# State-space stage: the first eight projected blocks in another order, the second group's decay masks built later, and its two segment halves parted by a projection

## The chip, the cores and the metric

The kernel runs on one core of one Trainium2 chip. The metric is the device time of one execution in microseconds (us). Five engines work side by side and meet only through semaphores: TensorE (PE in the profile), VectorE (DVE), ScalarE (ACT), GpSimd (POOL) and SyncE (SP), which here issues the loads.

## What is computed

A perceiver layer on 128 latent tokens of width 512: cross-attention, then a state-space (Mamba-2-like) mixer, then a sparse feed-forward, each behind a layer norm and a residual. The change lies wholly in the beginning of the mixer, whose reference reads, cut to what matters:

```python
proj = hidden_states @ in_proj_w.T              # gate 8192, x 8192, B 1024, C 1024, dt 128 columns
xc = conv_general_dilated(hBC, conv_w, ...) + conv_b      # 4 taps, per channel
hBC = silu(xc)                                            # x, B, C come out of this
dt = softplus(dt + dt_bias)
Lmat = exp(segment_sum(A * dt))                           # per head, 128 x 128, causal
Gm = einsum('bclhn,bcshn->bclsh', Cch, Bch)               # C times B, one for each of 8 groups
M = Gm * Lmat
Y_diag = einsum('bclsh,bcshp->bclhp', M, x * dt)
y = Y_diag + D * x
y = rmsnorm(y) * norm_w * silu(gate)
return y @ out_proj_w.T
```

With 128 tokens there is one chunk, so no state is carried over. There are 8 groups of 16 heads; one group has 1024 columns of x and 1024 of gate.

## The kernel before, in words

Everything is kept transposed (channels on partitions, tokens along the free axis). The input projection is done in **blocks** of 4 x 128 output channels (32 matmul records in the profile). A block is one slot of a ring of six weight buffers (1 MB each), loaded by SP in the order of use, and it goes into PSUM bank 0 or 1 in turn. `in_proj` (L1467) waits for its weights and for `proj_ev`, which ScalarE counts up each time it has read a block out of its bank, so a block can start when the block two before it has been read.

The mixer starts with a prologue of eight blocks, whose rows of the weight matrix are listed in `FIRST_IN`: group 0's two gate blocks and two x blocks, two B blocks and two C blocks (B and C serve all groups). From then on each group takes four blocks, which hold the x and gate of the next group: `project(g, j)` with j = 0, 1 for x and j = 2, 3 for gate.

What the other engines do with a block:

- A gate block: ScalarE applies silu from PSUM into `sg` (`gate_out`, L721).
- An x, B or C block: ScalarE copies it to `raw` and writes the last tap with the bias into `acc` (`raw_out`, L524 and four times L710); VectorE adds the other three taps with twelve instructions (`conv`, L1056) that read `raw` and `acc` in SBUF and then counts `taps` up; ScalarE applies silu into `xc` or `bc` (`conv_silu`, L717) and counts `silu_ok` up. There are two `raw`/`acc` pairs.

Decays of a group g: GpSimd writes the group's `a = A*dt` masked by causality into `at_hi`/`at_lo` with two selects (`steps_a(g)`, L499), PE sums them along the segment by a product with a triangular matrix, half a group (8 heads) at a time into banks 2 and 3 (`segments(g, b, half)`, L1478/L1479), ScalarE takes the exponential (`decay_exp`, L726), and VectorE multiplies with `gm` (`mask_decay`, L1071). There is one pair of banks, so a `segments` waits for the `decay_exp` of the one before it. `gm` is the product of C and B (PE, L1527, then masked on VectorE, L1113); it needs all six convolutions of the prologue (`silu_ok` 6).

`x_transposes(g)` (L1487) turns x to tokens on partitions in banks 4 and 5, VectorE scales it by dt (`x_times_dt`, L1076), `y_product(g)` (L1496) writes y over the same banks, and VectorE adds `D*x` (`skip_add`, L1084) and counts `y_ok` up, which the next `x_transposes` waits for. ScalarE squares y for the norm (`squares`, L733), VectorE multiplies it with the gate (`gated`, L1092), and `out_proj` (L1507) projects.

The order on every engine is the order of the code; nothing is scheduled by a planner. ScalarE's exp and silu lie in different function tables, and an `ACT_TABLE_LOAD` stands wherever it passes from one to the other. The first two groups are written out by hand, since the pipeline fills there; from group 1 on every engine runs `mamba_step`.

Of the kernel before, what the change touches and what calls it, by code (L numbers as in the profile page):

```python
# [22 lines left out]
ACT = mybir.ActivationFunctionType  # L23
# [3 lines left out]
T = 128  # L27
# [68 lines left out]
def build(nc, x, ctx_t, wq, wk, wv, wo, w_in, w_dt, w_out, conv_w, conv_b, dt_bias, a_log, d_skip,  # L96
          norm_w, c1, c2, w1, w2, w2_tail, out):
    with ExitStack() as ctx:
# [74 lines left out]
        with ExitStack() as st3:  # L173
# [24 lines left out]
            with ExitStack() as st4:  # L198
# [14 lines left out]
                raw = [sbuf(st4, f"raw{b}", [P, 4, T]) for b in range(2)]  # L213
                acc = [sbuf(st4, f"acc{b}", [P, 4, T]) for b in range(2)]
                xc = [sbuf(st4, "xc0", [P, TPG, T])]
# [66 lines left out]
        def stream(m):  # L282


            slot = (m + 2) % RING
            return slot, BEFORE[slot] + m // RING

        FIRST_IN = (0, 1, 16, 17, 32, 33, 34, 35)

        def step_chunk(g, j):  # L290

            slot, before = stream(8 + j)
            return slot, before + g
# [129 lines left out]
        def _(pool):  # L423
# [72 lines left out]
            def steps_a(g):  # L496

                for dst, src in ((at_hi[g % 2], a_hi), (at_lo[g % 2], a_lo)):
                    i = pool.affine_select(  # L499
                        out=dst[:], in_=src[:, g * HPG:g * HPG + HPG].bitcast(F32).unsqueeze(2).to_broadcast([P, HPG, T]),  # L500
                        compare_op=ALU.is_ge, fill=0.0, base=0, pattern=[[0, HPG], [1, T]],
                        channel_multiplier=-1)
                i.then_inc(at_ok, 1)
# [3 lines left out]
            pool.memset(c2_sb[:], 0.0).then_inc(zeroed, 1)  # L507
            pool.wait_ge(a_ok, 2)
            steps_a(0)
            steps_a(1)  # L510
            for g in range(GROUPS - 2):
                pool.wait_ge(seg_ps, 2 * g + 4)
# [10 lines left out]
        def _(act):  # L523
# [174 lines left out]
            act.wait_ge(const_in, 128)  # L698
            nc.scalar.activation(softplus[5][:], alog[:], ACT.Exp).then_inc(a_ok, 1)

            def raw_out(chunk, k, bank, tile):


                act.wait_ge(freed[chunk[0]], chunk[1] + 1)
                if not (isinstance(k, int) and k < 2):
                    act.wait_ge(taps, k - 1)
                    act.wait_ge(silu_ok, k - 1)
                copy(raw[bank][:], ps[:, bank, :].rearrange("p (c t) -> p c t", c=4))
                for i in range(4):
                    ins = nc.scalar.activation(acc[bank][:, i, :], ps[:, bank, i * T:i * T + T], ACT.Identity,  # L710
                                               bias=cb[:, bass.ds(tile + i, 1)],
                                               scale=cw[:, bass.ds(tile + i, 1), 3:4].rearrange("p a b -> p (a b)"))
                ins.then_inc(proj_ev, 1)

            def conv_silu(k, slot, dst):
                act.wait_ge(taps, k + 1)
                nc.scalar.activation(dst, acc[slot][:], ACT.Silu).then_inc(silu_ok, 1)  # L717

            def gate_out(chunk, bank, dst):
                act.wait_ge(freed[chunk[0]], chunk[1] + 1)  # L720
                nc.scalar.activation(dst, ps[:, bank, :].rearrange("p (c t) -> p c t", c=4),  # L721
                                     ACT.Silu).then_inc(proj_ev, 1)

            def decay_exp(g, b, half):
                act.wait_ge(seg_ps, 2 * g + half + 1)
                nc.scalar.activation(decay[b][:, 8 * half:8 * half + 8, :],  # L726
                                     ps[:, 2:4, :].rearrange("p a (h t) -> p (a h) t", t=T),
                                     ACT.Exp).then_inc(dec_ok, 1)
# [3 lines left out]
                act.wait_ge(sq_ok, g + 1)  # L732
                nc.scalar.activation(ysq[:], yv[:], ACT.Square).then_inc(ysq_ok, 1)  # L733

            gate_out(stream(0), 0, sg[0][:, 0:4, :])
            gate_out(stream(1), 1, sg[0][:, 4:8, :])
            raw_out(stream(2), 0, 0, 0)
            raw_out(stream(3), 1, 1, 4)
            conv_silu(0, 0, xc[0][:, 0:4, :])
            raw_out(stream(4), 2, 0, 64)  # L740
            conv_silu(1, 1, xc[0][:, 4:8, :])
            raw_out(stream(5), 3, 1, 68)
            conv_silu(2, 0, bc[:, 0:4, :])
            raw_out(stream(6), 4, 0, 72)
            conv_silu(3, 1, bc[:, 4:8, :])
            raw_out(stream(7), 5, 1, 76)
            conv_silu(4, 0, bc[:, 8:12, :])
            conv_silu(5, 1, bc[:, 12:16, :])
            decay_exp(0, 0, 0)

# [3 lines left out]
            raw_out(step_chunk(0, 1), 7, 1, 12)  # L754
            decay_exp(1, 1, 0)
            decay_exp(1, 1, 1)
            gate_out(step_chunk(0, 2), 0, sg[1][:, 0:4, :])
            conv_silu(6, 0, xc[1][:, 0:4, :])
            conv_silu(7, 1, xc[1][:, 4:8, :])
            gate_out(step_chunk(0, 3), 1, sg[1][:, 4:8, :])  # L760
            squares(0)
# [54 lines left out]
        def _(dve):  # L816
# [247 lines left out]
            def taps_of(q, k, slot, tile):  # L1064
                dve.wait_ge(proj_ev, q + 1)
                conv(k, slot, tile)
# [40 lines left out]
                nc.vector.tensor_tensor(sq_sum[:], sq_sum[:], ysq[:], ALU.add).then_inc(sq_ok, 1)  # L1107

            for k, tile in enumerate((0, 4, 64, 68, 72, 76)):
                taps_of(k + 2, k, k % 2, tile)  # L1110
            x_times_dt(0)
            dve.wait_ge(gm_ps, 1)
            nc.vector.tensor_tensor(gm[:], ps[:, 6:8, :].rearrange("p a (g t) -> p (a g) t", t=T),  # L1113
# [100 lines left out]
        def _(pe):  # L1214
# [296 lines left out]
            def project(g, j):  # L1511
                slot, before = step_chunk(g, j)
                in_proj(slot, before + 1, 4 * g + 8 + j, j % 2)
# [7 lines left out]

            x_transposes(0, 0)
            project(0, 0)
            project(0, 1)
            pe.wait_ge(silu_ok, 6)
            for g in range(GROUPS):
                ins = mm(ps[:, 6 + g // 4, (g % 4) * T:(g % 4 + 1) * T], bc[:, g, :], bc[:, 8 + g, :],  # L1527
                         start=True, stop=True)
            ins.then_inc(gm_ps, 1)
            segments(0, 0, 1)  # L1530
            project(0, 2)
            segments(1, 1, 0)
            segments(1, 1, 1)
            y_product(0, 0)
            project(0, 3)
# [142 lines left out]
```

## Time and profile before

| what | value |
|---|---|
| three timed runs | 661.26, 661.22, 659.51 us; median 661.22 |
| the profiled execution | 660.41 us, of it 657.9 us are the profile's span |
| PE busy in the span | 638.9 us, 97% |
| share of PE on the chain that ended last | 86% |
| the mixer, from its first block to the addition to the residual | 396.0 to 625.9 us of the span |

The span is what the records cover; the rest of the execution lies outside the engines' records. PE is the engine of the kernel: what matters is where it stands still, and who ended each standstill. The state-space prologue ends at about 452 us, where PE enters the loop body for group 1.

### The profile page before, as it was taken

Reading aid. Unit: us, or ns where it says so; the run is one execution under the profiler, and the core shown is the slowest. Engines: PE = TensorE matmul, PEld = TensorE weight load, DVE = VectorE, ACT = ScalarE, POOL = GpSimd, SP = SyncE. Lnnn points to the kernel's source line nnn. Section 1 sums busy time; section 2 is a strip of 40 time slices with the busy share of each in tenths; the row PEclk is TensorE's granted clock in tenths of the full one; section 3 lists DMA queues with packets and bytes.
Section 4 is the critical chain, followed back from the end, with each engine's and each line's share of the span. In section 5 each row is a group of like instructions: output and inputs, shape, how many; then the busy total and the mean of one; then the engine's idle time right before and its main releaser. Section 6 shows DMA issues by size and latency. Waiting matters only on the chain.

```text
span 657.9 us, 12479 instructions
## 1 busy us (share of the span) xinstructions
PE 638.9 (97%) x4212; PEld 546.6 (83%) x4212; DVE 451.4 (69%) x1056; ACT 362.3 (55%) x711; POOL 203.9 (31%) x150
## 2 busy tenths in 40 slices
PE   7999999999999999999999999998999999999998
PEld 6888888898899989998999879987788797797473
DVE  3533143787788878787888665979975856758873
ACT  3413115777787778767877744767354444447210
POOL 0000000644674478447755454003320220200000
PEclk9999999999999999999999999999999999999999
DMA  7611002226254442625242656674657658597600
GB/s 254 273 64 62 4 0 69 78 69 196 73 153 121 135 137 73 195 67 193 60 130 67 229 236 166 246 281 151 237 214 269 249 201 298 212 350 294 250 1 16
DMA packets 27224, 104.80 MB, mean 159 GB/s; under 512 B 7424, under 2 KB 7808, under 8 KB 17584
## 3 DMA queue, kind: packets, MB, share of 16 engines
q1 hardware_dynamic: 26608, 103.23, 45.9%
q10 hardware_dynamic: 576, 1.05, 0.5%
q8 instruction: 23, 0.38, 0.2%
q14 instruction: 17, 0.14, 0.1%
HBM read 86.30 MB, written 0.26 MB: 132 GB/s over the span
## 4 chain that ended last, share of the span: by engine, by line
PE 86%; DVE 4%; POOL 4%; ACT 3%; issue 1%; DMA 1%; SPq 0%; ACTq 0%; DVEq 0%
PE ps L1467 19%; PE ps L1225 14%; PE ps L1226 14%; PE ps L1227 14%; PE ps L1507 8%; PE ps L1358 4%; PE ps L1302 3%; POOL pt_lo L430 3%; PE ps L1496 2%; PE ps L1617 2%; PE ps L1580 1%; DVE acc L1056 1%; DMA ring<-wk_dram 1%; POOL k_lo L430 1%; PE ps L1487 1%
## 5 line engine op out<-in xcount | busy, mean ns | idle before, releaser
L1467 PEld LDWEIGHTS ps<-norm_t,ring 128*128 128x128 f32 x1152 | 131.5, 192 | 4.8 <-issue 4.1
L1467 PE MATMUL ps<-norm_t,ring 128*128 128x128 f32 x1152 | 133.1, 276 | 0.0
L1056 DVE SCALAR_TENSOR_TENSOR acc<-raw,cw,acc 128x127 f32<-128x127 f32 (+2 forms) x240 | 85.9, 432 | 23.1 <-ACT acc L710 22.2
L430 POOL TENSOR_TENSOR pt_lo<-far_t,pt_hi 128x512 fp32r<-128x512 f32 (+1 forms) x75 | 87.3, 1183 | 37.9 <-ACT pt_hi L524 37.7
L1225 PE MATMUL ps<-pt_hi,v_hi 128*128 128x256 f32 x272 | 84.6, 311 | 3.0 <-POOL pt_lo L430 2.7
L524 ACT ACTIVATE pt_hi<-ps 128x512 fp32r<-128x512 f32 (+1 forms) x69 | 41.0, 596 | 67.1 <-PE ps L1358 67.0
L1227 PE MATMUL ps<-pt_lo,v_hi 128*128 128x256 f32 x272 | 76.6, 282 | 0.0
L1226 PE MATMUL ps<-pt_hi,v_lo 128*128 128x256 f32 x272 | 76.5, 281 | 0.0
L915 DVE TENSOR_SCALAR_CACHE_REDUCE prob_near<-ps 128x512 f32<-128x512 f32 x64 | 44.2, 691 | 24.4 <-PE ps L1227 22.6
L817 DVE TENSOR_TENSOR pt_lo<-ps,pt_hi 128x512 fp32r<-128x512 f32 (+1 forms) x69 | 47.4, 688 | 18.9 <-ACT pt_hi L524 17.6
L499 POOL TENSOR_SCALAR_AFFINE_SELECT at_hi<-a_hi 128x2048 fp32r<-128x2048 f32 x8 | 17.0, 2130 | 136.6 <-PE ps L1479 125.5
L1225 PE MATMUL ps<-k_hi,q_hi 128*128 128x512 f32 (+1 forms) x160 | 58.7, 367 | 0.7 <-DVE k_lo L817 0.3
L1226 PE MATMUL ps<-k_hi,q_lo 128*128 128x512 f32 (+1 forms) x160 | 59.2, 370 | 0.0
L1227 PE MATMUL ps<-k_lo,q_hi 128*128 128x512 f32 (+1 forms) x160 | 58.7, 367 | 0.0
L915 DVE TENSOR_SCALAR_CACHE_REDUCE prob_far<-ps 128x512 f32<-128x512 f32 (+1 forms) x96 | 51.0, 554 | 11.2 <-PE ps L1227 11.2
L1225 PEld LDWEIGHTS ps<-pt_hi,v_hi 128*128 128x128 f32 x272 | 51.6, 190 | 7.5 <-POOL pt_lo L430 5.4
L430 POOL TENSOR_TENSOR wo_lo<-ring,wo_hi 128x1024 fp32r<-128x1024 f32 x15 | 36.2, 2410 | 66.7 <-ACT wo_hi L524 66.7
L1507 PE MATMUL ps<-ring,ug 128*128 128x512 f32 x128 | 56.7, 594 | 0.0
L430 POOL TENSOR_TENSOR v_lo<-v_all,v_hi 128x768 fp32r<-128x768 f32 (+1 forms) x12 | 20.7, 1752 | 115.8 <-ACT v_hi L524 115.8
L1226 PEld LDWEIGHTS ps<-pt_hi,v_lo 128*128 128x128 f32 x272 | 51.6, 190 | 1.6
L1227 PEld LDWEIGHTS ps<-pt_lo,v_hi 128*128 128x128 f32 x272 | 51.2, 188 | 0.0
L602 ACT ACTIVATE prob_far<-prob_far,neg_max 128x512 f32<-128x512 f32 x64 | 48.9, 767 | 3.4 <-DVE neg_max L919 2.7
(205 smaller groups left out, 1311.0 us busy)
## 6 DMA issues: line engine op xcount, KB each, us to landing
ring<-w_in_dram SPq DMA_DIRECT2D x36, 1024.0 KB, 4.9
far_t<-blocks_t SPq DMA_DIRECT2D x240, 72.0 KB, 2.0
ring<-w_out_dram SPq DMA_DIRECT2D x16, 1024.0 KB, 4.9
ring<-wq_dram SPq DMA_DIRECT2D x8, 1024.0 KB, 5.1
ring<-wo_dram SPq DMA_DIRECT2D x8, 1024.0 KB, 6.9
w_sb<-w_dram SPq DMA_DIRECT2D x4, 896.0 KB, 9.1
ring<-ctx_t_dram SPq DMA_DIRECT2D x3, 1024.0 KB, 6.8
ring<-w_dram SPq DMA_DIRECT2D x3, 1024.0 KB, 8.6
```

The source lines that it names most:

```text
L430: sub = lambda dst, a, hi: pool.tensor_tensor(dst, a, hi, ALU.subtract)
L524: copy = lambda dst, src: nc.scalar.activation(dst, src, ACT.Copy)
L602: nc.scalar.activation(prob(b, h, lo, hi), prob(b, h, lo, hi), ACT.Exp, bias=neg_max[:, b, h:h + 1], accum_out=part_sum[:, b, h, i:i + 1]) ...
L817: sub = lambda dst, a, hi: nc.vector.tensor_tensor(dst, a, hi, ALU.subtract)
L915: nc.vector.tensor_scalar(prob(b, h, lo, hi), ps[:, c % 4, 0:hi - lo], SCALE, None, ALU.mult, ALU.max, accum_out=chunk_max[:, b, h, i:i + ...
L1056: ins = nc.vector.scalar_tensor_tensor(a[:, i, back:], r[:, i, 0:T - back], cw[:, bass.ds(tile + i, 1), 3 - back:4 - back].rearrange("p a ...
L1225: mm(dst, a_hi_, b_hi_, start=first, stop=False)
L1226: mm(dst, a_lo_, b_hi_, start=False, stop=False)
L1227: return mm(dst, a_hi_, b_lo_, start=False, stop=last)
L1358: ins = nc.tensor.transpose(ps[:, 4 + u % 2, at:at + P], prob(b, h, kt * P, kt * P + P), ident[:])
L1467: ins = mm(ps[:, bank, t * T:t * T + T], w[:, t, c, :], norm_t[:, c, :], start=(c == 0), stop=(c == NC - 1))
L1507: ins = mm(ps[:, 6, :], ug[b][:, 4 * i + t, :], w[:, t, :], start=(first and i == 0 and t == 0), stop=(last and i == 1 and t == 3))
```

## The change

Five edits:

1. `FIRST_IN` lists the prologue's blocks in the order x, x, gate, B, B, C, C, gate instead of gate, gate, x, x, B, B, C, C. Banks, ring slots and PE's instructions stay the same. ScalarE's code follows, so `raw_out` now takes the `raw`/`acc` pair and the bank apart (an odd block can be in pair 0).
2. VectorE's convolutions wait for the changed count of blocks read.
3. GpSimd builds group 1's masked steps (`steps_a(1)`) only after the six convolutions of the prologue (`taps` 6).
4. PE computes `gm` and group 0's second segment half before the second x block of group 1 instead of behind it, and group 1's two segment halves have the first gate block of group 1 between them.
5. ScalarE takes `conv_silu(6)` ahead of `gate_out(step_chunk(0, 2))`.

```diff
-        FIRST_IN = (0, 1, 16, 17, 32, 33, 34, 35)
+        FIRST_IN = (16, 17, 0, 32, 33, 34, 35, 1)
...
             steps_a(0)
+            pool.wait_ge(taps, 6)
             steps_a(1)
...
-            gate_out(stream(0), 0, sg[0][:, 0:4, :])
-            gate_out(stream(1), 1, sg[0][:, 4:8, :])
-            raw_out(stream(2), 0, 0, 0)
-            raw_out(stream(3), 1, 1, 4)
+            raw_out(stream(0), 0, 0, 0)
+            raw_out(stream(1), 1, 1, 4)
+            gate_out(stream(2), 0, sg[0][:, 0:4, :])
             conv_silu(0, 0, xc[0][:, 0:4, :])
-            raw_out(stream(4), 2, 0, 64)
+            raw_out(stream(3), 2, 0, 64, 1)
             conv_silu(1, 1, xc[0][:, 4:8, :])
-            raw_out(stream(5), 3, 1, 68)
+            raw_out(stream(4), 3, 1, 68, 0)
             conv_silu(2, 0, bc[:, 0:4, :])
-            raw_out(stream(6), 4, 0, 72)
+            raw_out(stream(5), 4, 0, 72, 1)
             conv_silu(3, 1, bc[:, 4:8, :])
-            raw_out(stream(7), 5, 1, 76)
+            raw_out(stream(6), 5, 1, 76, 0)
             conv_silu(4, 0, bc[:, 8:12, :])
+            gate_out(stream(7), 1, sg[0][:, 4:8, :])
             conv_silu(5, 1, bc[:, 12:16, :])
...
+            conv_silu(6, 0, xc[1][:, 0:4, :])
             gate_out(step_chunk(0, 2), 0, sg[1][:, 0:4, :])
-            conv_silu(6, 0, xc[1][:, 0:4, :])
             conv_silu(7, 1, xc[1][:, 4:8, :])
...
-                taps_of(k + 2, k, k % 2, tile)
+                taps_of(k + (k > 1), k, k % 2, tile)
...
             project(0, 0)
-            project(0, 1)
             pe.wait_ge(silu_ok, 6)
             for g in range(GROUPS):
                 ins = mm(ps[:, 6 + g // 4, (g % 4) * T:(g % 4 + 1) * T], bc[:, g, :], bc[:, 8 + g, :],
                          start=True, stop=True)
             ins.then_inc(gm_ps, 1)
             segments(0, 0, 1)
+            project(0, 1)
+            segments(1, 1, 0)
             project(0, 2)
-            segments(1, 1, 0)
             segments(1, 1, 1)
```

How it moves instructions. First PE, behind the product C times B: `at_hi0` are group 0's masked steps and `at_hi1` group 1's, `ring5` is the second x block of group 1 and `ring0` its first gate block. Before:

```order
L1478 MATMUL ps<-at_hi0,upper_r 128x512 [waits at_ok,dec_ok]
L1479 MATMUL ps<-at_lo0,upper_r 128x512
L1478 MATMUL ps<-at_hi0,upper_r 128x512
L1479 MATMUL ps<-at_lo0,upper_r 128x512
L1467 MATMUL ps<-norm_t,ring0 128x128 [waits proj_ev,landed0]
L1467 MATMUL ps<-norm_t,ring0 128x128 x15
L1478 MATMUL ps<-at_hi1,upper_r 128x512 [waits at_ok,dec_ok]
L1479 MATMUL ps<-at_lo1,upper_r 128x512
L1478 MATMUL ps<-at_hi1,upper_r 128x512
L1479 MATMUL ps<-at_lo1,upper_r 128x512
L1478 MATMUL ps<-at_hi1,upper_r 128x512 [waits at_ok,dec_ok]
L1479 MATMUL ps<-at_lo1,upper_r 128x512
```

and in the changed kernel (its lines have other numbers: L1469 is `in_proj`, L1480 and L1481 are `segments`):

```order
L1481 MATMUL ps<-at_lo0,upper_r 128x512
L1480 MATMUL ps<-at_hi0,upper_r 128x512
L1481 MATMUL ps<-at_lo0,upper_r 128x512
L1469 MATMUL ps<-norm_t,ring5 128x128 [waits proj_ev,landed5]
L1469 MATMUL ps<-norm_t,ring5 128x128 x15
L1480 MATMUL ps<-at_hi1,upper_r 128x512 [waits at_ok,dec_ok]
L1481 MATMUL ps<-at_lo1,upper_r 128x512
L1480 MATMUL ps<-at_hi1,upper_r 128x512
L1481 MATMUL ps<-at_lo1,upper_r 128x512
L1469 MATMUL ps<-norm_t,ring0 128x128 [waits proj_ev,landed0]
L1469 MATMUL ps<-norm_t,ring0 128x128 x15
L1480 MATMUL ps<-at_hi1,upper_r 128x512 [waits at_ok,dec_ok]
```

The block of `ring5` has moved from ahead of the product into the gap between group 0's and group 1's segments, and the block of `ring0` into the gap between the halves of group 1; the two groups of `at_hi1` no longer stand back to back.

Second ScalarE, at the entry of the prologue; `freed2` to `freed5` and `freed0` are the signals that PE is through with the first to fifth block. Before:

```order
L721 ACT_TABLE_LOAD
L721 ACTIVATE sg0<-ps 128x512 [waits freed2]
L721 ACTIVATE sg0<-ps 128x512 [waits freed3]
L524 ACTIVATE raw0<-ps 128x512 [waits freed4]
L710 ACTIVATE acc0<-ps,cb,cw 128x128 x4
L524 ACTIVATE raw1<-ps 128x512 [waits freed5]
L710 ACTIVATE acc1<-ps,cb,cw 128x128 x4
L717 ACTIVATE xc0<-acc0 128x512 [waits taps]
L524 ACTIVATE raw0<-ps 128x512 [waits silu_ok,taps,freed0]
```

and in the changed kernel:

```order
L525 ACTIVATE raw0<-ps 128x512 [waits freed2]
L712 ACTIVATE acc0<-ps,cb,cw 128x128 x4
L525 ACTIVATE raw1<-ps 128x512 [waits freed3]
L712 ACTIVATE acc1<-ps,cb,cw 128x128 x4
L723 ACT_TABLE_LOAD
L723 ACTIVATE sg0<-ps 128x512 [waits freed4]
L719 ACTIVATE xc0<-acc0 128x512 [waits taps]
L525 ACTIVATE raw0<-ps 128x512 [waits silu_ok,taps,freed5]
L712 ACTIVATE acc0<-ps,cb,cw 128x128 x4
```

The two x blocks are now read out at the first and second block's end (`freed2`, `freed3`) instead of at the third's and fourth's, the load of the silu table has moved behind them, and the first B block (`raw0` after `xc0`) is the fourth block instead of the fifth, still behind the first convolution (`taps`, `silu_ok`).

## Rows read from the trace of the kernel before

**Rows 1.** Part 1 of the page: busy time, share of the span, instructions

```profile
PE 638.9 (97%) x4212; PEld 546.6 (83%) x4212; DVE 451.4 (69%) x1056; ACT 362.3 (55%) x711; POOL 203.9 (31%) x150
```

**Rows 2.** The chain that ended last, at the prologue's end: start us, us, what

```profile
435.56 1.23 DVE gm L1113
436.79 3.14 DVE acc L1056 x12
...
440.13 2.36 DVE decay L1071 x2
442.49 6.63 DVE acc L1056 x12
...
449.26 2.17 DVE yv L1084 x8
```

**Rows 3.** PE in order of time: start, us, instruction xcount, [idle before <-releaser]

```profile
426.43 7.31 PE L1467 MATMUL ps<-norm_t,ring 128*128 128x128 f32 x64
433.57 1.95 PE L1527 MATMUL ps<-bc 128*128 128x128 f32 x16
435.28 0.47 PE L1478 MATMUL ps<-at_hi,upper_r 128*128 128x512 f32 x1
...
436.29 3.73 PE L1467 MATMUL ps<-norm_t,ring 128*128 128x128 f32 x32
...
442.06 0.50 PE L1478 MATMUL ps<-at_hi,upper_r 128*128 128x512 f32 x1 [1.11 <-ACT decay L726]
...
443.19 1.97 PE L1496 MATMUL ps<-decay,xdt 128*64 128x128 f32 x32
...
451.56 1.06 PE L1487 MATMUL ps<-ident,xc 128*128 128x128 f32 x8 [2.63 <-DVE yv L1084]
...
456.88 0.48 PE L1478 MATMUL ps<-at_hi,upper_r 128*128 128x512 f32 x1
```

**Rows 4.** DVE in order of time, the prologue's first half

```profile
403.18 0.29 DVE L817 TENSOR_TENSOR a_lo<-a_f,a_hi 128x128 fp32r<-128x128 f32 x1
408.99 5.24 DVE L1056 SCALAR_TENSOR_TENSOR acc<-raw,cw,acc 128x127 f32<-128x127 f32 x12 [5.51 <-ACT acc L710]
...
421.11 9.96 DVE L1056 SCALAR_TENSOR_TENSOR acc<-raw,cw,acc 128x127 f32<-128x127 f32 x36 [0.15 <-DVE acc L1056]
```

**Rows 5.** POOL in order of time: steps of groups 0, 1 and 2

```profile
403.55 2.01 POOL L499 TENSOR_SCALAR_AFFINE_SELECT at_hi<-a_hi 128x2048 fp32r<-128x2048 f32 x1 [11.12 <-DVE a_lo L817]
...
409.42 2.06 POOL L499 TENSOR_SCALAR_AFFINE_SELECT at_lo<-a_lo 128x2048 fp32r<-128x2048 f32 x1
443.33 2.07 POOL L499 TENSOR_SCALAR_AFFINE_SELECT at_hi<-a_hi 128x2048 fp32r<-128x2048 f32 x1 [31.86 <-PE ps L1479]
```

**Rows 6.** POOL and DVE in order of time, in the attention

```profile
365.45 2.41 POOL L430 TENSOR_TENSOR wo_lo<-ring,wo_hi 128x1024 fp32r<-128x1024 f32 x1 [6.60 <-ACT wo_hi L524]
...
366.36 0.69 DVE L817 TENSOR_TENSOR pt_lo<-ps,pt_hi 128x512 fp32r<-128x512 f32 x1
```

**Rows 7.** ACT in order of time: read-outs of the prologue and its end

```profile
415.55 1.50 ACT L710 ACTIVATE acc<-ps,cb,cw 128x128 f32<-128x128 f32 x4
...
422.68 1.50 ACT L710 ACTIVATE acc<-ps,cb,cw 128x128 f32<-128x128 f32 x4
...
449.74 0.58 ACT L721 ACTIVATE sg<-ps 128x512 f32<-128x512 f32 x1
451.45 1.06 ACT L733 ACTIVATE ysq<-yv 128x1024 f32<-128x1024 f32 x1 [1.13 <-DVE yv L1084]
...
454.12 1.28 ACT L726 ACT_TABLE_LOAD   x1
455.41 1.03 ACT L726 ACTIVATE decay<-ps 128x1024 f32<-128x1024 f32 x1
```

**Rows 8.** SP's queue in order of time, and loads: KB, median us to landing

```profile
434.56 0.87 SPq L324 DMA_DIRECT2D ring<-w_out_dram  x2
...
ring<-w_out_dram SPq DMA_DIRECT2D x16, 1024.0 KB, 4.9
```

More of the change, by code:

```diff
@@ L699, in _, with raw_out @@
             nc.scalar.activation(softplus[5][:], alog[:], ACT.Exp).then_inc(a_ok, 1)
-            def raw_out(chunk, k, bank, tile):
+            def raw_out(chunk, k, slot, tile, bank=None):
+                bank = slot if bank is None else bank
                 act.wait_ge(freed[chunk[0]], chunk[1] + 1)
@@ L707, in raw_out @@
                     act.wait_ge(silu_ok, k - 1)
-                copy(raw[bank][:], ps[:, bank, :].rearrange("p (c t) -> p c t", c=4))
+                copy(raw[slot][:], ps[:, bank, :].rearrange("p (c t) -> p c t", c=4))
                 for i in range(4):
-                    ins = nc.scalar.activation(acc[bank][:, i, :], ps[:, bank, i * T:i * T + T], ACT.Identity,
+                    ins = nc.scalar.activation(acc[slot][:, i, :], ps[:, bank, i * T:i * T + T], ACT.Identity,
                                                bias=cb[:, bass.ds(tile + i, 1)],
```

## The prediction, made before the changed kernel ran

> **What bounds the kernel now.** I read the page's busy times first: PE is busy for 638.9 us of 657.9 [rows 1], so only what keeps PE waiting can be won. The chain that ended last comes next: it runs on PE nearly everywhere in the mixer, but between 435.6 and 451.6 us it runs on VectorE (gm, convolution 6, two masks, convolution 7, skip_add), without a gap of note [rows 2]. PE's timeline gives the price: it stands still for 1.11 us before the second half of group 1's segments, released by ScalarE's decay, and for 2.63 us before group 1's x_transposes, released by VectorE's skip_add [rows 3]. That is 3.74 us in all; behind 451.56 the prologue's shape has no further idle on PE, and each piece follows its predecessor. The third thing to see is GpSimd against VectorE. Convolution 0 took 5.24 us for its twelve instructions, while three convolutions later on took 9.96, or 3.32 each [rows 4]; the last select of group 1's steps lay over it until 411.48 [rows 5]. Convolution 7 took 6.63 us, over group 2's selects from 443.33 on [rows 2, 5]. An instruction of VectorE with both inputs in SBUF gets about one turn for each select and otherwise stands; one with an input in PSUM took its 0.69 us inside a GpSimd subtraction of 2.41 us [rows 6]. x_times_dt, the product that makes gm, and skip_add read PSUM; convolutions and masks don't.
>
> **The head: x first.** PE's eight blocks and their times stay; a block is half of the 7.14 us between 426.43 and 433.57, so 3.57 us [rows 3]. The two x blocks are ready 7.1 us earlier, but VectorE is busy with dt until 403.47 and GpSimd's two selects for group 0 follow at once (403.55, some 4 us, to 407.6) [rows 4, 5]. So convolution 0 starts at 403.5, gets two or three instructions in, and then needs what it needed behind 411.48 before: until 408.99 + 5.24 = 414.23, 2.75 us. It ends at 410.3, 3.9 us earlier than before. This is also where the new order has a danger. The first B block is now the fourth and its read-out stands behind convolution 0 and its silu; before, 415.55 + 1.50 = 417.05 lay 2.8 us behind convolution 0's end [rows 7], so now it is done at 413.1. The sixth block needs that bank; it starts at 426.43 less 0.9 for the transposes, three blocks and a segment half of 1.0, at 413.8 [rows 3]. Margin 0.7 us. I take no wait. Convolutions 1 to 4 follow at 3.32 each, to 423.6. Convolution 5 needs the second C block, now the seventh, whose read-out ends when the seventh block's did before, at 422.68 + 1.50 = 424.18 [rows 7]; it ends at 427.5. Before it ended at 421.11 + 9.96 = 431.07 [rows 4]: 3.6 us earlier.
>
> **PE's new order.** It moves no work, only places. project(0, 0) ends at 430.0. gm needs silu_ok 6, at 428.2 (427.5 and a silu), so it starts at once, 3.57 us earlier than before. Group 0's second half starts at 431.7 and needs the first decay, which ScalarE has at 428.2 + 1.3 for the table + 1.0 = 430.5 [rows 7]: margin 1.2. project(0, 1) runs from 432.7 to 436.3, group 1's first half to 437.3, project(0, 2) to 440.9, where the second half starts. What it waits for, the decay of the first half, is at the earliest 437.4 + 1.0; ScalarE first reads out project(0, 1) (436.5 to 438.5), so it is there at 439.5, margin 1.4. So the wait of 1.11 goes: a block of 3.57 us now lies over it. y_product starts 1.11 earlier, at 442.1, and x_transposes(1) could start at 451.56 - 2.63 - 1.11 = 447.8.
>
> **Group 1's steps later.** GpSimd builds them at 427.6 to 431.7 and PE wants them at 436.3, margin 4.6. What VectorE does there is x_times_dt (PSUM) and then waits for gm: nothing that the selects can hold. Nothing else is queued behind the new wait but group 2's steps, which wait for PE at 442.2 anyway.
>
> **VectorE behind gm.** gm's product ends at 431.7, its mask starts at 432.0, and from there the work to convolution 7 took 442.49 - 435.56 = 6.9 us [rows 2]: convolution 7 at 438.9 (its input is ready at 438.5), its end at 442.1. The masks end at 438.9, 3.2 us before y_product wants them. Group 2's selects start 0.14 us behind the end of the segments (443.33 against 443.19) [rows 3, 5], so at 442.2 to 442.3: convolution 7 just gets out of their way, with 0.2 us to spare. skip_add then waits for y_product (442.1 + 1.97) and takes 2.17: it ends at 446.5 [rows 2, 3], 1.3 us before PE can start x_transposes(1). Silu 7 lies behind the table load and ends at 446.2. So the 2.63 us go too.
>
> **What is late next.** The decay for group 2's first half. ScalarE comes to it by gate_out(3), squares, the copy for the feed-forward, a table load and the exponential. squares no longer waits for skip_add, but for gate_out, and that for PE: PE's end 447.8 + 0.2, a silu (0.5), then 455.41 + 1.03 - 451.45 = 5.0 [rows 7] gives 453.5. PE wants it 456.88 - 451.56 = 5.32 us behind its start of x_transposes [rows 3], at 453.1. So a new wait of about 0.4 us. Its bounds: nothing, if the tail overlaps by a little more, and 0.8. Then the sum is -1.11 - 2.63 + 0.4 = -3.3 us. Behind that point all is tied to PE and moves with it.
>
> The same chain is where a rule speaks against the change. Between the table load's start at 454.12 and the exponential's at 455.41 lie 1.29 us [rows 7]. The Trainium skill (ScalarE: Activation LUTs, What ACT_TABLE_LOAD costs) puts a switch at 1.28 us and a drain of 1.38, some 2.66 us in all. By that rule the decay would come 1.4 us later and the sum would be about -1.9; by the row it is -3.3. The row disagrees with the rule for this chain, and I follow the row.
>
> **Queues and loads.** The block order only changes which rows of the weights are fetched: the same sizes in the same slots. ring5's next load starts when project(0, 1) ends, 2.7 us later than now, and the two loads of w_out behind it in SP's queue (at 434.56) move to about 437.3; a load lands in 4.9 us [rows 8]. project(1, 1), the next to use ring5, runs behind y_product(1), 10 us later than that. Cost nothing.
>
> **The sum.** The profiled execution is 660.41 us with a span of 657.9; less 3.3 this is 657.1. It lies 0.8 below the median of the three runs, from which one comes to 657.9. I say 657.4, its own range 656.5 to 658.2.
>
> **Rivals.** 0.3% is about what a measurement of this kernel can tell from no change, 2.0 us.
>
> *The selects catch convolution 7 (chance 0.12).* Its margin is 0.2 us. If VectorE is a little late, each of the last instructions takes a select's whole time; convolution 7 ends at 446.4, skip_add at 448.7, x_transposes(1) at 448.8. Saved: 451.56 - 448.8 = 2.7; and the new wait for the decay is gone, since PE is later. If x_times_dt and gm's mask were held by group 1's selects too (against rows 6), it is 2.4. The time would be 658.1.
>
> *Half of it (0.06).* Convolution 0 is held for one select more (2.0 us), ends at 412.4 and the sixth block waits 1.3 us. Saved 2.0, less some repetition of it: 1.2 to 2.0, about 659.
>
> *The table's drain (0.02).* As worked out, a switch that costs 1.4 us more than the row: saved 1.9, about 658.8. Every switch in rows 7 speaks against it.
>
> *Nothing happens (0.05).* VectorE's chain is as late as before relative to PE, because the six convolutions don't end earlier: for that convolution 5 would have to end at 431. Time 660.4 to 661.2.
>
> *Slower (0.05).* The x-first order ties PE to convolution 0: from 411.1 on, each us that it ends later holds the sixth block and all behind it by one. It takes back all when it ends at 414.4, and the kernel is slower from there. If the two selects and VectorE hold each other more than they did here, say with three more holds of 2.0 us, it ends at 416.4: 2.0 us slower, 662.5. For it speaks that VectorE and GpSimd start within 0.1 us of each other here; against it, that rows 4 and 5 show the selects keep their 2.01 and 2.06 us and only two of them run.
>
> **How the numbers follow.** The forecast has 0.70. Faster by over 0.3% are the forecast and the first rival: 0.82. Within 0.3% lie half, drain and nothing: 0.13. Slower 0.05. For the range I take the lowest of the runs less the whole 3.74, 655.8, and at the upper end the median less 1.2, 660.0: this leaves out nothing of the forecast and the first three rivals, and the last two.
>
> **What would show it.** In the changed profile: convolution 0 starts at 403.5 and ends near 410.3; convolution 5 ends near 427.5; no idle on PE before either half of group 1's segments; the selects of group 1 between 427.6 and 431.7 with no convolution stretched; x_transposes(1) at 447.8 without idle; a wait of about 0.4 us on ScalarE's decay before group 2's second half, at 453.5 instead of 456.88. I am wrong if PE waits at the sixth block, if convolution 7 has an instruction of 2 us, or if that last wait is much over 0.4.

## The result

| | runs | median | range |
|---|---|---|---|
| before | 4 | 661.24 us | 659.51 to 661.43 |
| changed | 4 | 655.43 us | 654.60 to 656.01 |

The ratio is 0.9919, with a 95% interval of 0.9908 to 0.9931: the changed kernel is faster by 5.4 us (4.6 to 6.1); the two medians lie 5.8 us apart. The forecast was 657.4 us with a range of 655.8 to 660.0, so the direction was right, but the gain was larger than the 3.3 us of its sum, and the median lies 0.4 us below the range. A second set of the same two kernels gave 0.9924 (0.9910 to 0.9937), 5.0 us.

The profiled execution of the changed kernel took 654.6 us with a span of 652.9, 5.0 less than the 657.9 of the trace before. The 660.41 us that stand beside that trace belong to another execution: its span is on record as 658.7 us at a mean granted clock of 0.997, while the trace has 657.9 at 1.000. In all runs that have both figures, time and span are 1.7 to 1.8 us apart, so the traced execution of the kernel before took about 659.6 us (an estimate).

PE in order of time in the changed kernel, against [rows 3]:

```profile
394.78 21.60 PE L1469 MATMUL ps<-norm_t,ring 128*128 128x128 f32 x192
...
424.30 1.04 PE L1489 MATMUL ps<-ident,xc 128*128 128x128 f32 x8
425.17 3.74 PE L1469 MATMUL ps<-norm_t,ring 128*128 128x128 f32 x32
...
431.45 3.74 PE L1469 MATMUL ps<-norm_t,ring 128*128 128x128 f32 x32
...
439.45 0.48 PE L1480 MATMUL ps<-at_hi,upper_r 128*128 128x512 f32 x1
...
440.55 1.97 PE L1498 MATMUL ps<-decay,xdt 128*64 128x128 f32 x32
442.45 3.84 PE L1469 MATMUL ps<-norm_t,ring 128*128 128x128 f32 x32
446.13 1.04 PE L1489 MATMUL ps<-ident,xc 128*128 128x128 f32 x8
...
451.84 0.50 PE L1480 MATMUL ps<-at_hi,upper_r 128*128 128x512 f32 x1 [0.16 <-ACT decay L728]
```

No row of PE from 394.78 to 446.13, those left out included, has an idle before it. The two waits of before [rows 3] are gone: the second half of group 1's segments (439.45) follows the gate block, and x_transposes of group 1 (446.13) follow project(0, 3). The one wait left is the last row's, on ScalarE's decay. Group 0's x_transposes of the kernel before, which [rows 3] leave out, are

```profile
425.55 1.04 PE L1487 MATMUL ps<-ident,xc 128*128 128x128 f32 x8
```

From one x_transposes to the next it was 451.56 - 425.55 = 26.01 us before; it is 446.13 - 424.30 = 21.83 now, 4.18 less. From there to group 2's second half it was 5.32 [rows 3] and is 5.71, 0.39 more. The net gain of this path is 3.79 us.

VectorE and GpSimd over the same time in the changed kernel, against [rows 2, 4, 5]:

```profile
402.14 6.70 DVE L1058 SCALAR_TENSOR_TENSOR acc<-raw,cw,acc 128x127 f32<-128x127 f32 x12
...
422.95 3.22 DVE L1058 SCALAR_TENSOR_TENSOR acc<-raw,cw,acc 128x127 f32<-128x127 f32 x12 [0.64 <-ACT acc L712]
...
430.73 1.22 DVE L1115 TENSOR_TENSOR gm<-ps,causal 128x1024 f32<-128x1024 f32 x1 [3.19 <-PE ps L1528]
...
437.58 3.21 DVE L1058 SCALAR_TENSOR_TENSOR acc<-raw,cw,acc 128x127 f32<-128x127 f32 x12
442.57 2.16 DVE L1086 SCALAR_TENSOR_TENSOR yv<-xc,dskip,ps 128x128 f32<-128x128 f32 x8 [1.78 <-PE ps L1498]
```

```profile
402.29 2.05 POOL L499 TENSOR_SCALAR_AFFINE_SELECT at_hi<-a_hi 128x2048 fp32r<-128x2048 f32 x1 [11.13 <-DVE a_lo L819]
404.30 2.05 POOL L499 TENSOR_SCALAR_AFFINE_SELECT at_lo<-a_lo 128x2048 fp32r<-128x2048 f32 x1
426.30 2.00 POOL L499 TENSOR_SCALAR_AFFINE_SELECT at_hi<-a_hi 128x2048 fp32r<-128x2048 f32 x1 [19.95 <-DVEq L1064]
...
440.70 2.00 POOL L499 TENSOR_SCALAR_AFFINE_SELECT at_hi<-a_hi 128x2048 fp32r<-128x2048 f32 x1 [10.44 <-PE ps L1481]
```

Times here are 1.26 us earlier than in the profile of before for a reason outside the change (below), so 402.14 stands for 403.4. Convolution 0 ends at 408.84, convolution 5 at 426.17. Convolution 7 has 3.21 us instead of 6.63 [rows 2] (6.7 from the start of its first instruction) and ends at 440.79; group 2's selects begin at 440.70, over its last instruction only. skip_add (442.57) now waits for y_product instead of PE for it.

### The profile page after: what moved, and what is told of

It is laid out like the page before. It is cut to its first block, busy times and chain, and to the rows that moved or that the text cites. A ratio compares the mean times of both kernels' runs of the same rounds, so it can differ in the third digit from the quotient of the medians.

```text
span 652.9 us, 12479 instructions
## 1 busy us (share of the span) xinstructions
PE 638.7 (98%) x4212; PEld 546.7 (84%) x4212; DVE 449.1 (69%) x1056; ACT 362.1 (55%) x711; POOL 202.8 (31%) x150
## 4 chain that ended last, share of the span: by engine, by line
PE 88%; POOL 4%; ACT 3%; issue 2%; DVE 2%; DMA 1%; ACTq 0%; SPq 0%; DVEq 0%
PE ps L1469 19%; PE ps L1227 14%; PE ps L1228 14%; PE ps L1229 14%; PE ps L1509 8%; PE ps L1360 4%; PE ps L1304 3%; POOL pt_lo L430 3%; PE ps L1498 2%; PE ps L1619 2%; PE ps L1582 1%; DMA ring<-wk_dram 1%; POOL k_lo L430 1%; PE ps L1480 1%; PE ps L1481 1%
## 5 line engine op out<-in xcount | busy, mean ns | idle before, releaser
L1469 PEld LDWEIGHTS ps<-norm_t,ring 128*128 128x128 f32 x1152 | 131.7, 192 | 4.9 <-issue 4.1
L1469 PE MATMUL ps<-norm_t,ring 128*128 128x128 f32 x1152 | 133.2, 276 | 0.0
L1058 DVE SCALAR_TENSOR_TENSOR acc<-raw,cw,acc 128x127 f32<-128x127 f32 (+2 forms) x240 | 83.4, 424 | 18.8 <-ACT acc L712 18.2
```

Of the source, the lines that this page charges most:

```text
L1058: ins = nc.vector.scalar_tensor_tensor(a[:, i, back:], r[:, i, 0:T - back], cw[:, bass.ds(tile + i, 1), 3 - back:4 - back].rearrange("p a ...
L1469: ins = mm(ps[:, bank, t * T:t * T + T], w[:, t, c, :], norm_t[:, c, :], start=(c == 0), stop=(c == NC - 1))
```

## The experiments

For all runs two distances on PE's timeline are compared, because they don't depend on how the kernel started: A from group 0's x_transposes to group 1's, B from there to group 2's second segment half (all start to start).

| kernel | A us | B us | span of the profile us |
|---|---|---|---|
| before | 26.01 | 5.32 | 657.9 |
| before, again | 26.01 | 6.86 | 658.7 |
| changed | 21.83 | 5.71 | 652.9 |
| changed, again | 21.83 | 5.72 | 654.4 |
| block_order_only | 26.01 | 6.93 | 660.2 |
| pe_order_only | 24.31 | 5.72 | 656.6 |
| together | 23.22 | 5.72 | 655.2 |
| no_swap | 21.83 | 5.71 | 653.9 |
| no_defer | 21.83 | 5.71 | 658.3 |
| copy_early | 21.83 | 5.31 | 653.3 |
| filled | 26.01 | 5.32 | 657.8 |
| selects_later | 23.21 | 5.71 | 655.4 |

Behind B all of them agree within about 0.1 us (197.3 us to the start of the last product). What A and B leave of the spans' differences lies in the kernel's start, and in no_defer also in the prologue ahead of A (experiment 5).

**1. The kernel before against itself, and the changed kernel again.** No edit.

> The kernel before, unchanged, against itself. The change saved 5.8 us by the medians, but between the start of the mixer and the second half of group 2's segments the two profiles differ by only 3.8 us; the other 1.2 us lie in the first 17 us of the span, where nothing was changed (the second piece of the first loads is split on VectorE at 10.15 instead of 11.36 us). Theory A (the start is chance): executions of the same program differ by 1 to 2 us for that reason alone, so two sets of runs of the same kernel agree within 0.2% and the profile of this one can show the second split anywhere between 10 and 11.5 us. Theory B (the two programs start differently): this one again shows it at 11.3 to 11.4 and its times lie at 661, with a ratio of 1.000 within 0.001.

> The changed kernel, unchanged. Theory A (the start is chance, the change is worth what the prologue shows): the ratio to the kernel before moves to about 0.9943 (3.8 us saved), and the start of the profile differs from the first one's. Theory B (something in the start belongs to the change): ratio again 0.992 and the second split again near 10.15 us. In both the prologue takes the same time as in the first profile: x_transposes of group 0 to those of group 1 in 21.8 us, a wait of 0.4 us before group 2's second segment half.

The kernel before against itself: 1.0008 (0.9999 to 1.0017). The changed one: 0.9924 (0.9910 to 0.9937). The start is chance: the distance to the 61st product on PE, inside the first 19 us, was 18.32 and 17.59 us in the two profiles of before, 17.08 and 18.65 in those of the changed kernel. So the 1.26 us between the first two profiles are no part of the change. But theory A did not hold as I put it: the ratio did not move to 0.9943, it stayed 5.0 us. What I had not expected lay in B of the profile of before_again, 6.86 us where it had been 5.32. PE in order of time:

```profile
450.86 1.94 PE L1487 MATMUL ps<-ident,xc 128*128 128x128 f32 x8 [2.63 <-DVE yv L1084]
...
454.23 3.73 PE L1467 MATMUL ps<-norm_t,ring 128*128 128x128 f32 x32
457.72 0.48 PE L1478 MATMUL ps<-at_hi,upper_r 128*128 128x512 f32 x1
```

and the stretches of it, with busy times and PEclk, the granted clock:

```profile
core 0: us, PE busy (x) PEld busy (x) DVE busy (x) ACT busy (x) POOL busy (x), PEclk, DMA share, GB/s
448.00:451.00 3.00, 0.36 (x4) 0.20 (x3) 2.85 (x11) 1.37 (x3) 0.00 (x0) 0.95 0.53 131
451.00:454.00 3.00, 3.00 (x12) 2.71 (x13) 3.00 (x3) 2.98 (x3) 0.00 (x0) 0.50 0.54 224
454.00:457.00 3.00, 3.00 (x27) 2.96 (x26) 3.00 (x10) 1.72 (x2) 0.00 (x0) 0.98 0.00 0
```

The eight transposes take 1.94 us instead of 1.06 [rows 3], and between 451 and 454 us the granted clock is 0.50, 1.2 GHz instead of 2.4. It fell in the last tenths of a microsecond of PE's idle time before them. In the first profile of before the same wait of 2.63 us stood [rows 3] and the clock in that stretch was 1.00:

```profile
451.00:454.00 3.00, 2.44 (x18) 2.29 (x19) 3.00 (x5) 2.55 (x2) 0.00 (x0) 1.00 0.74 306
```

The profile of block_order_only (experiment 3) has the same wait, 2.65 us in it. There the clock held for the transposes and fell about 1.3 us after PE had resumed (mean clock in the column behind PE's busy time):

```profile
454.00:457.00 3.00, 3.00 (x14) 0.52 0.03 8
```

So the wait seems to have a second price, paid in some executions and not in others; experiment 2 tests that.

**2. The wait filled with work.** PE computes throw-away products while it waits; nothing else is changed.

```diff
             project(0, 3)
+            pe.wait_ge(gm_ok, 1)
+            for _ in range(11):
+                mm(ps[:, 7, 0:P], ident[:], ident[:], start=True, stop=True)
             mamba_step(1, 0, 1, True)
```

> The kernel before with eleven throw-away products of ident with ident (into bank 7, which is free there) on PE between project(0, 3) and group 1's x_transposes, about 2.3 us of work inside the wait of 2.8 us; nothing else is changed and no result uses them. In three profiles with that wait, two show the granted clock at one half (1.2 GHz) for 3.4 us right behind it, and there group 1's x_transposes to group 2's second segment half take 6.9 us instead of 5.3; the profiles without the wait never show it. Theory A (the wait costs its own length and, in most executions, 1.5 us more through the clock): filled, x_transposes(1) starts where it did, 26.0 us behind group 0's, the clock stays at full and the following piece takes 5.3 us in the profile; the timed runs are 1.0 to 1.5 us faster than the kernel before, ratio about 0.998. Rival (the clock's drop there is chance, or the spread comes from the start of the kernel alone): ratio 1.000, and spread as before. If the eleven products end behind VectorE's skip_add, x_transposes(1) starts later and the gain is less by that.

Ratio 0.9985 (0.9976 to 0.9994), 1.0 us faster (0.4 to 1.6) although A is 26.01 as before. The spans and mean granted clocks of the timed runs, sorted:

```
filled (12 runs): 657.1 657.3 657.4 657.6 657.7 657.7 657.8 657.9 657.9 658.0 658.0 658.2   clock 0.997 to 1.000
before (17 runs): 657.1 657.2 657.2 658.0 658.5 658.5 658.6 658.9 659.0 659.1 659.1 659.2 659.2 659.3 659.5 659.5 659.5   clock 0.972 to 1.000
```

The fastest are alike; what filling removes are the runs above 658.2, thirteen of seventeen. The mean clocks go with it: the four fastest runs of before have 1.000, seven of the thirteen others 0.995, and no run of filled is below 0.997. A mean of 0.997 is what the one fall in the profile of filled makes; that one lies in the kernel's start, at 9 to 12 us, where nothing was edited. PE in the profile of filled:

```profile
448.63 2.62 PE L1551 MATMUL ps<-ident 128*128 128x128 f32 x22
451.44 1.06 PE L1487 MATMUL ps<-ident,xc 128*128 128x128 f32 x8 [0.19 <-DVE yv L1084]
```

The wait of 2.63 us has become work and 0.19 us of idle, the transposes take 1.06, and B is 5.32, which alone would not tell it from the first profile of before; the timed runs do. That is theory A's result: PE's idleness there, not the length of the path, costs about 1 us on average.

**3. One half of the change at a time.** block_order_only has PE's order of before; pe_order_only is the kernel before with PE's new order.

```diff
 block_order_only, against the changed kernel
             project(0, 0)
+            project(0, 1)
...
             segments(0, 0, 1)
-            project(0, 1)
-            segments(1, 1, 0)
             project(0, 2)
+            segments(1, 1, 0)
             segments(1, 1, 1)
```

> The changed kernel with PE's order of before (both x blocks, then gm, group 0's second half, first gate block, group 1's halves back to back); block order, the later steps of group 1 and ScalarE's swap stay. Theory A (the block order only gives room, PE's order must use it): the six convolutions end 3.6 us earlier, but gm starts where it did before, the wait of 1.1 us before group 1's second half comes back, convolution 7 meets group 2's selects again, and x_transposes(1) starts within 0.3 us of before: no gain. Rival (the earlier x is the main thing): at least 2 us of the 4.2 us are kept.

> The kernel before with PE's new order alone (gm and group 0's second half ahead of the second x block, group 1's halves parted by the first gate block); the block order stays gate, gate, x, x, B, B, C, C and group 1's steps are built at once. Theory A (PE's order needs the earlier convolutions): gm waits 1.8 us for the sixth silu, group 0's second half another 0.6 us for the first decay; the waits before group 1's second half and, mostly, before x_transposes(1) go. x_transposes(1) starts 0.7 to 1.7 us earlier than before. Rival (PE's order is all): x_transposes(1) starts 3.7 to 4.2 us earlier.

block_order_only keeps nothing: A is 26.01. VectorE shows why, first the row of gm in the kernel before and then block_order_only:

```profile
435.56 1.23 DVE L1113 TENSOR_TENSOR gm<-ps,causal 128x1024 f32<-128x1024 f32 x1 [3.12 <-PE ps L1527]
```


```profile
436.23 1.23 DVE L1115 TENSOR_TENSOR gm<-ps,causal 128x1024 f32<-128x1024 f32 x1 [6.76 <-PE ps L1529]
...
443.08 6.70 DVE L1058 SCALAR_TENSOR_TENSOR acc<-raw,cw,acc 128x127 f32<-128x127 f32 x12
```

VectorE stood idle for 6.76 us before gm (3.12 in the kernel before), and then ran the same chain as before, convolution 7 under the selects included (6.70 us). The six convolutions ended earlier for nothing. (Its span, the longest of all, also holds the fall of the clock in B and a standstill of 1.29 us at 21.67, in the kernel's start.) pe_order_only reaches 24.31, 1.70 of the 4.18, at the upper end of what was expected:

```profile
431.80 2.05 PE L1526 MATMUL ps<-bc 128*128 128x128 f32 x16 [1.64 <-ACT bc L717]
434.14 0.50 PE L1478 MATMUL ps<-at_hi,upper_r 128*128 128x512 f32 x1 [0.28 <-ACT decay L726]
...
449.86 1.04 PE L1487 MATMUL ps<-ident,xc 128*128 128x128 f32 x8
```

The product for gm waits for the sixth silu and the segments for the first decay, 1.8 and 0.4 us, but both waits further back are gone. Convolution 7 took 3.21 us here too, from 441.72 to 444.93, with group 2's selects from 444.43 on: with gm ahead of the second x block it is out of the selects' way. So PE's order frees both waits, and the earlier convolutions take away what that order would wait for at gm. The block order is worth the other 2.5 us, and only together with PE's order.

**4. The segment halves together again, gate and silu swapped back.**

```diff
 together, against the changed kernel
             project(0, 1)
-            segments(1, 1, 0)
             project(0, 2)
+            segments(1, 1, 0)
             segments(1, 1, 1)
 no_swap, against the changed kernel
-            conv_silu(6, 0, xc[1][:, 0:4, :])
             gate_out(step_chunk(0, 2), 0, sg[1][:, 0:4, :])
+            conv_silu(6, 0, xc[1][:, 0:4, :])
```

> The changed kernel with group 1's segment halves back to back behind the first gate block, gm and group 0's second half still ahead of the second x block. Theory A: PE waits for the first half's decay as in the kernel before, 1.1 to 1.3 us, and x_transposes(1) starts by that much later than in the changed kernel. Rival (VectorE sets x_transposes(1), so the wait is covered): no difference at x_transposes(1).

> The changed kernel with gate_out of the first gate block of group 1 ahead of conv_silu(6) again, as before. Theory A (neither is late: the last silu ends at 444.6, PE wants it at 446.1): no difference on PE. Rival (conv_silu order frees something): group 1's x_transposes start at least 0.1 us later.

Together costs 1.39 us in A: the row of the second half carries the same idle as before.

```profile
439.44 0.48 PE L1480 MATMUL ps<-at_hi,upper_r 128*128 128x512 f32 x1
...
441.73 0.50 PE L1480 MATMUL ps<-at_hi,upper_r 128*128 128x512 f32 x1 [1.11 <-ACT decay L728]
...
442.86 1.97 PE L1498 MATMUL ps<-decay,xdt 128*64 128x128 f32 x32
```

Here VectorE was not late: the wait stands on PE's own path and shows in full at x_transposes(1). The swap is worth nothing (21.83 and 5.71).

**5. Group 1's steps not held back.**

```diff
             steps_a(0)
-            pool.wait_ge(taps, 6)
             steps_a(1)
```

> The changed kernel without the wait that holds back group 1's steps, so GpSimd runs four selects in a row beside convolution 0. Theory A (selects hold a VectorE instruction with both inputs in SBUF for their whole length, and the x-first order ties PE to convolution 0): convolution 0 gets one instruction in for each select and ends near 412.5 us instead of 408.8, the first B block is read out at 415.3, the sixth block waits 2.7 us, and x_transposes(1) starts 2.7 us later than in the changed kernel. Rival (the margin of the sixth block is real slack and takes it): less than 0.5 us later.

GpSimd, VectorE and PE of this run:

```profile
403.46 2.06 POOL L499 TENSOR_SCALAR_AFFINE_SELECT at_hi<-a_hi 128x2048 fp32r<-128x2048 f32 x1 [11.13 <-DVE a_lo L818]
...
409.48 2.05 POOL L499 TENSOR_SCALAR_AFFINE_SELECT at_lo<-a_lo 128x2048 fp32r<-128x2048 f32 x1
```

```profile
403.31 10.19 DVE L1057 SCALAR_TENSOR_TENSOR acc<-raw,cw,acc 128x127 f32<-128x127 f32 x12
```

```profile
395.95 18.03 PE L1468 MATMUL ps<-norm_t,ring 128*128 128x128 f32 x160
416.47 5.28 PE L1468 MATMUL ps<-norm_t,ring 128*128 128x128 f32 x32 [2.49 <-ACT acc L711]
```

Convolution 0 takes 10.19 us beside four selects, 6.70 beside two, 3.2 alone. Its end at 413.50 puts the read-out of the first B block at 416.33, and the sixth block waits 2.49 us for it; it starts 2.66 us late. Then it takes 5.28 us for its 32 products instead of 3.7: the clock has fallen here too.

```profile
core 0: us, PE busy (x) PEld busy (x) DVE busy (x) ACT busy (x) POOL busy (x), PEclk, DMA share, GB/s
...
414.00:417.00 3.00, 0.53 (x2) 0.56 (x3) 2.87 (x11) 2.26 (x7) 0.00 (x0) 0.86 1.01 415
417.00:420.00 3.00, 3.00 (x18) 3.00 (x17) 2.99 (x12) 2.58 (x6) 0.00 (x0) 0.57 0.57 235
```

From the mixer's start to group 0's x_transposes it is 33.72 us instead of 29.51: 2.7 as theory A had it and 1.5 for the clock, which it did not have. The wait on `taps` is therefore a needed part of the change: without it the profiled execution took 659.98 us, against 654.60 and 656.09 in the two profiles of the changed kernel.

**6. The copy taken out of the last wait.**

```diff
             decay_exp(1, 1, 0)
+            act.wait_ge(stack_in, 96)
+            copy(c2_st[:], c2_sb[:]).then_inc(c2h_ok, 1)
             decay_exp(1, 1, 1)
...
             squares(0)
-            act.wait_ge(stack_in, 96)
-            copy(c2_st[:], c2_sb[:]).then_inc(c2h_ok, 1)
```

> The changed kernel with the copy of c2_sb to c2_st moved on ScalarE from behind the squares of group 0 to between the two decays of group 1, where ScalarE was idle for 2.53 us. Theory A (the new wait of 0.4 us is ScalarE's chain gate, squares, copy, table, decay): the decay for group 2 comes 1.7 us earlier, PE's project(1, 0) is followed by the segments without a wait, group 1's x_transposes to group 2's second segment half take 5.3 instead of 5.7 us, and the kernel gains 0.4 us. Rival (the wait is only the signal's way or PE's switch from one product to the other): no difference.

B is 5.31 instead of 5.71, theory A. ScalarE goes from the squares straight to the table:

```profile
447.69 1.05 ACT L735 ACTIVATE ysq<-yv 128x1024 f32<-128x1024 f32 x1
448.75 1.28 ACT L728 ACT_TABLE_LOAD   x1
450.05 1.02 ACT L728 ACTIVATE decay<-ps 128x1024 f32<-128x1024 f32 x1
```

The timed runs: 655.23 us median (655.04 to 655.29) beside 655.68 for the changed kernel in the same set, ratio to before 0.9921 (0.9907 to 0.9934). The 0.4 us show in the profile; the timed difference alone would not carry them. It is the best version found.

**7. Only group 2's selects moved.** After that one question was open: how much of the old wait was the selects over convolution 7.

```diff
                 pool.wait_ge(seg_ps, 2 * g + 4)
+                if g == 0:
+                    pool.wait_ge(taps, 8)
                 steps_a(g + 2)
```

(in the kernel before, with nothing of the change)

> The kernel before with one wait more and nothing of the change: GpSimd starts group 2's two selects only when convolution 7 has ended (taps 8), instead of at the end of group 1's segments, so they no longer lie over convolution 7 (which took 6.6 us there and takes 3.2 alone). Theory A (of the wait of 2.8 us before group 1's x_transposes all was the selects' doing): convolution 7 ends at 445.7 us, skip_add follows y_product and ends near 447.6, x_transposes(1) starts with PE's own end at 448.8, 23.2 us behind group 0's instead of 26.0; group 2's steps are then ready at 449.9, so its first half waits some 0.2 us and the second half 0.4 us for the decay; with the clock's share, 3.3 to 4.0 us are saved, ratio about 0.9945. Rival (VectorE is late at gm already, by the two x blocks that PE projects ahead of it, so that the selects only fill slack): x_transposes(1) stays within 0.5 us of before, ratio 1.000.

Ratio 0.9944 (0.9931 to 0.9958), 3.7 us, with A 23.21 and B 5.71, all as theory A said.

```profile
442.16 3.21 DVE L1058 SCALAR_TENSOR_TENSOR acc<-raw,cw,acc 128x127 f32<-128x127 f32 x12
445.51 2.16 DVE L1086 SCALAR_TENSOR_TENSOR yv<-xc,dskip,ps 128x128 f32<-128x128 f32 x8
447.59 4.14 DVE L1073 TENSOR_TENSOR decay<-decay,gm 128x1024 f32<-128x1024 f32 x2
```

```profile
444.84 3.84 PE L1469 MATMUL ps<-norm_t,ring 128*128 128x128 f32 x32
448.51 1.04 PE L1489 MATMUL ps<-ident,xc 128*128 128x128 f32 x8
```

Convolution 7 takes 3.21 us, and x_transposes(1) follow PE's own block without idle. The masks behind (4.14 us instead of 2.35) are held by the selects instead, and PE's rows show no wait for them. One wait in one place gives three quarters of what the five edits give.

## Why the forecast was right, and where its size was off

**The head (right).** Convolution 0 was to begin with the selects and to end 3.9 us earlier; it began at 402.14 and ended at 408.84, which is 410.1 in the times of before, against 410.3 forecast. The sixth block did not wait. Convolution 5's end, 427.4 in those times, was forecast at 427.5.

**PE's new order (right).** Every margin held, and experiment 3 shows that the order is what turns the earlier convolutions into time; experiment 4 shows the parted halves at 1.39 us.

**The two waits (right place, short by 0.3 us).** x_transposes(1) were forecast at 447.8 and started at 446.13, which is 447.4 in the times of before. The forecast took 1.11 and 2.63 us from the idle in [rows 3]. These rows count from the modelled end of a product. project(0, 3) stands with 3.84 us in both profiles, but in the changed one the next instruction starts 3.68 us behind its start; a segment's last product stands with 0.39 or 0.40, and the next one starts 0.23 later. So each wait is longer by 0.16 than its row says. Together 1.27 and 2.79 are 4.06 of the 4.18. The last 0.1 us lie mostly in PE's own pieces: what follows a block starts 3.49 us after it where that is a segment half, and 3.57 us where it is another block or gm's product, and the new order has one more of the first kind.

**The new wait (right).** Forecast 0.4 us on the decay of group 2, measured 0.39 in B, and experiment 6 removes it by shortening ScalarE's chain. The row of that chain also held against the rule that the prediction cites: in copy_early the table load at 448.75 is followed by the exponential at 450.05, 1.30 us later and not 2.66 (the Trainium skill, ScalarE: Activation LUTs, What ACT_TABLE_LOAD costs). The two other loads in the prologue's second half of the trace before are alike: 431.80 to 433.10 and 444.34 to 445.63.

**The lock of VectorE by the selects (right, and larger than its place in the text).** The forecast treated it as a danger to a margin of 0.2 us. That margin did not hold: the selects came at 440.70, 442.0 in the times of before and not 442.2 to 442.3, and convolution 7 ended 0.1 us into them. It took no harm because its last instruction had started at 440.44, which is luck; but skip_add then waited 1.78 us for y_product, so one instruction held by a select, some 1.75 us longer (an estimate: 6.70 less 3.21, halved), would not have moved PE either. Experiment 7 shows that this collision was the whole of the 2.8 us in the kernel before. The Trainium skill (SBUF — State Buffer, Who interferes with whom) says that an instruction of VectorE with two inputs in SBUF contends with one of GpSimd that reads SBUF, and calls the ports that they share an exclusive lock. The traces agree: 3.2, 6.7 and 10.2 us for the same convolution beside none, two and four selects.

**The sum (mis-sized).** The forecast's step "less 3.3 this is 657.1" left out that a standing PE can lose its clock. The term was 3.3 us; the path gave 3.79 in the profiles, and the clock about 1.0 more (0.4 to 1.6, experiment 2): 4.8, against 5.0 (4.2 to 5.9) in the second set. The profile it was worked out from could not show that, since it was one of the executions in which the clock stayed at 1.00 behind the wait, and the forecast set its lower end by the waits' own length. The first set's ratio, 5.4 (4.6 to 6.1), holds that too; what lies between is within the spread of the start, 1.6 us between the profiles. The mean clocks part the two shares once more. Taking all sets together, the runs at a mean clock of 1.000 have an average span of 657.5 us before (9 of 53 runs), 657.6 filled (6 of 12) and 653.6 changed (4 of 9): without any fall of the clock the change is worth 3.9 us, which is the path.

The base of the sum was off as well. It set 660.41 us beside the span of 657.9, but these are two executions; the traced one took about 659.6, and less 3.3 that is 656.3, not 657.1. The first set's profiles then add up: 659.6 less 3.79 for the path and 1.26 for the start is 654.6, as measured. That the range reached down to 655.8 is owed to the waits' full length taken from the lowest run, not to a term for the clock or the start; that the time missed its lower end by only 0.4 us is no merit of the sum.

Of the rivals, none happened; the rival that ended slower had the right mechanism, as experiment 5 shows, held off by the wait on `taps`.

## What to carry to other kernels

Look at which engine's instruction runs over the last wait's chain, and what shares its way to SBUF: moving two selects of GpSimd by 2.5 us was worth 3.7 us, more than the reordering of the matrix work alone (1.7 us in A, less 0.4 in B). Reordering producers pays only when the consumer's order takes it up; in A the two halves here were worth 0 and 1.7 us alone, and 4.2 together. When a wait of TensorE is priced, several executions should be looked at with their granted clock: a wait may cost half as much again in other executions than in the one profiled (1.5 us on top of 2.8 here).

## What the hardware showed that was not expected

- A wait of 2.8 us of PE in the middle of steady work was followed by a granted clock of 0.50 (1.2 GHz) in two of three profiles with it (B 6.86 and 6.93 us against 5.32), and one of 2.66 us in the only profile with that (experiment 5). Each of these falls cost some 1.5 us. Waits of 1.3 us, and the two of 1.8 and 0.4 us in pe_order_only, showed no such stretch in the prologue. But the length of the wait alone doesn't decide it. In the first 13 us of the kernel the clock fell in four of the twelve profiles (filled, pe_order_only, together, selects_later), during or soon after idle rows of 1.78 to 2.38 us, and it didn't fall at one of 1.89 in the second profile of the changed kernel. In selects_later, a row of PE and a stretch of it with the granted clock behind the busy time:

```profile
8.27 0.57 PE L1227 MATMUL ps<-ctx_hi,wk_hi 128*128 128x512 f32 x1 [2.05 <-DVE ctx_lo L819]
```

```profile
9.00:12.00 3.00, 3.00 (x8) 0.50 1.01 391
```

These early falls cost little: the spans of filled average 657.8 us at a mean clock of 0.997 and 657.6 at 1.000. What decides between a fall and none stays open.
- GpSimd's select and a VectorE instruction with two SBUF inputs take turns by whole instructions: each 2.0 us select let one convolution instruction through, whose row then shows 2.1 us instead of 0.35, as this one beside group 0's first select in the changed kernel:

```profile
402.40 2.09 DVE L1058 SCALAR_TENSOR_TENSOR acc<-raw,cw,acc 128x127 f32<-128x127 f32 x1
```

VectorE instructions with one PSUM input ran undisturbed: the eight of skip_add took 2.16 us at 442.57, beside the two selects that begin at 440.70, and 2.17 without [rows 2].
